# Ten of layer 2's 22 filtered adjacency tiles made during layer 1, two multiplied in the flow ahead of it; a ring of four; roots on GpSimd

## What is computed

```python
# layer 1: three rounds, A = adj scaled by the square roots of the row sums
h1 = x @ W1 + b1
n1 = _layernorm(jax.nn.relu(A @ h1) + h1, g1, be1)
...                                    # two more rounds of the same
# layer 2: only the 700 largest values of a row are kept; seldom more than 700 are there
sim = jnp.tanh(adj * simlar)           # simlar is adj itself
filt = sim * (adj > 0).astype(sim.dtype)
...
h2 = jnp.tanh(h @ W_proj + b_proj)
feat = jax.nn.relu(new_adj @ (h2 @ W_gcn) + b_gcn)
```

## Time and profile before

| | |
|---|---|
| time, median of 3 runs | 2290.98 us (2286.65 to 2292.18) |
| the profiled execution | 2291.57 us, of it the span 2289.7 us |
| PE busy | 1947.9 us, 85% of the span |
| DVE busy | 1574.2 us, 69% |
| ACT busy | 1111.3 us, 49% |
| POOL busy | 443.3 us, 19% |
| DMA | 389.10 MB, mean 170 GB/s |
| granted clock of TensorE | 0.934 mean |

### The profile page before, as it was taken

One profiled execution on the slowest core, in us unless ns is written; L12 is line 12 of the kernel. 1 busy time (PEld: TensorE's weight loads), 2 busy tenths in 40 slices (PEclk: granted clock), 3 DMA queues, 4 the chain that ended last, 5 costly groups with the idle time before them and its releaser, 6 DMA issues.

```text
span 2289.7 us, 42272 instructions
## 1 busy us (share of the span) xinstructions
PE 1947.9 (85%) x15872; PEld 1314.7 (57%) x15872; DVE 1574.2 (69%) x3183; ACT 1111.3 (49%) x2198; POOL 443.3 (19%) x455
## 2 busy tenths in 40 slices
PE   6999296899999999749966698669967999999788
PEld 3877263688888887637744577557754222222343
DVE  6866665655555577746667888645567999999555
ACT  7555275523223244427745677346545223232654
POOL 0000474100000022137741000057620000000000
PEclk9999697999999999969987899879988999999899
DMA  6999367556566589556754567433332343232000
GB/s 197 315 343 328 122 151 163 210 199 246 219 230 243 220 324 404 191 191 218 231 165 133 148 168 179 164 98 93 85 110 73 115 122 90 82 90 85 0 21 29
DMA packets 236971, 389.10 MB, mean 170 GB/s; under 512 B 20640, under 2 KB 189216, under 8 KB 221025
## 3 DMA queue, kind: packets, MB, share of 16 engines
q1 hardware_dynamic: 211972, 333.86, 44.4%
q0 software_dynamic: 15296, 43.88, 7.3%
q10 hardware_dynamic: 9504, 8.65, 1.2%
HBM read 304.55 MB, written 81.78 MB: 169 GB/s over the span
## 4 chain that ended last, share of the span: by engine, by line
PE 51%; DVE 27%; ACT 8%; DMA 8%; issue 4%; POOL 2%; SPq 1%; ACTq 0%; DVEq 0%; POOLq 0%
DVE BIG L2819 7%; PE ps L1078 6%; PE ps L1080 6%; PE ps L1079 6%; PE ps L283 5%; PE ps L284 4%; PE ps L285 4%; PE ps L2320 4%; PE ps L2641 4%; DMA BIG<-in_adjT 3%; PE ps L2647 2%; PE ps L2322 2%; DMA X<-rows_split,idxg 2%; DVE BIG L1735 2%; DVE BIG L1743 2%
## 5 line engine op out<-in xcount | busy, mean ns | idle before, releaser
L1078 PE MATMUL ps<-R,BIG 128*128 128x256 f16 (+1 forms) x1764 | 486.1, 276 | 13.4 <-DVE BIG L1110 8.6
L1080 PE MATMUL ps<-R,BIG 128*128 128x256 f16 (+1 forms) x1764 | 483.5, 274 | 0.0
L1079 PE MATMUL ps<-R,BIG 128*128 128x256 f16 x1764 | 483.4, 274 | 0.0
L2641 PE MATMUL ps<-BIG 128*64 128x452 f32 x1056 | 230.9, 558 | 23.9 <-DVE BIG L2819 20.1
L1078 PEld LDWEIGHTS ps<-R,BIG 128*128 128x128 f16 x1764 | 171.9, 97 | 41.3 <-DVE BIG L1110 9.1
L2819 DVE SCALAR_TENSOR_TENSOR BIG<-BIG 128x904 f32<-128x904 f32 x176 | 192.4, 1155 | 1.6
L1079 PEld LDWEIGHTS ps<-R,BIG 128*128 128x128 f16 x1764 | 173.8, 98 | 21.5
L1080 PEld LDWEIGHTS ps<-R,BIG 128*128 128x128 f16 x1764 | 172.0, 98 | 24.5
L2703 ACT ACTIVATE BIG<-X,BIG 128x64 f32<-128x64 f32 x264 | 70.2, 337 | 232.8 <-PE ps L2647 232.7
L2641 PEld LDWEIGHTS ps<-BIG 128*64 128x64 f32 x1056 | 64.4, 136 | 186.4 <-issue 131.1
L2320 PE MATMUL ps<-BIG,X 128*128 x464 | 155.6, 382 | 9.6 <-DVE X L2379 9.6
(11 more groups left out here) (419 smaller groups left out, 4489.8 us busy)
## 6 DMA issues: line engine op xcount, KB each, us to landing
BIG<-adj_split SPq DMA_DIRECT2D x63, 1376.0 KB, 6.5
BIG<-in_adjT SPq DMA_DIRECT2D x42, 1408.0 KB, 10.8
BIG<-in_adj SPq DMA_DIRECT2D x22, 1408.0 KB, 9.2
BIG<-in_adjT SPq DMA_DIRECT2D x66, 452.0 KB, 3.3
adj_split<-BIG SPq DMA_DIRECT2D x21, 1376.0 KB, 10.9
XX<-in_f SPq DMA_DIRECT2D x70, 256.0 KB, 7.9
experts_split<-XX SPq DMA_DIRECT2D x64, 256.0 KB, 4.4
BIG<-experts_split SPq DMA_DIRECT2D x16, 1024.0 KB, 13.0
```

The costliest lines, as they stand in the source:

```text
L1078: pe.matmul(out[:, 0:n], pr[:, 0, k, :], h[:, k, 0:n], start=start, stop=False)
L1079: pe.matmul(out[:, 0:D], pr[:, 0, k, :], l[:, k, 0:D], start=False, stop=False)
L1080: return pe.matmul(out[:, 0:n], pr[:, 1, k, :], h[:, k, 0:n], start=False, stop=stop)
L2641: pe.matmul(ps[rs, 2 * (h // 2) + c, 0:CW], self.G[:, u, h * HF:(h + 1) * HF], self.PT[:, u, h, cs], start=start, stop=stop)
```

## The change

The tiles of layer 2 are cut in two kinds, `AHEAD` (ten) and `LATE` (twelve). The filter of the AHEAD tiles, which needs only `adjT`, is done in runs 1 and 2 of P1: raw load to slot 5, square on DVE at tile m, tanh on ACT at m+1, high part on ACT and low part on DVE at m+2 into slot 4, and a store to the new DRAM tensor `filter_split`. For that the ring of P1 shrinks from six slots to four, loads waiting for three tiles' lead, and the counting passes move to other places (15 still in runs 1 and 2). P1's roots in runs 1 and 2 go from ACT to POOL, and ACT loads the table with tanh before run 1 and the one with Ln and Exp at the end of run 2. In C1, SP loads tiles 0 to 3 ready-made behind the transfers of rows 6, 9, 12 and 15, and PE multiplies tiles 0 and 1 in its steps from 10 on, block pair by block pair as the features come (`early`). P2 loads the other AHEAD tiles and filters only the twelve LATE ones. The unused branch gets the same ten tiles.

```diff
+RING = 4
+AHEAD = (0, 1, 2, 3, 5, 7, 9, 13, 15, 18)
+LATE = tuple(t for t in range(KT) if t not in AHEAD)
+SQUARES = tuple(4 * i + 2 for i in range(len(AHEAD)))
+COUNTS = tuple(m for m in range(2 * KT) if m % 6 in (1, 3)) + tuple(range(2 * KT + 2, 3 * KT, 3))
...
         class C1:
             def sp(self, sp, filter):
                 after(sp, self.experts, W[2], *self.before)
-                expert_rows(sp, self.st)
+                expert_rows(sp, self.st, {6: lambda: filter.part_load(sp, 0), 9: lambda: filter.part_load(sp, 1),
+                                          12: lambda: filter.part_load(sp, 2), 15: lambda: filter.part_load(sp, 3)})
...                                                            # C1.pe
+                    if i >= 10:
+                        beside.early(pe, i - 10)
...                                                            # C1.act
-                    if i == PR + 5:
-                        filter.first_part(act, 0)
...
         class P1:
             def sp(self, sp):
                 for n in range(3 * KT + 3):
-                    if n < 6:
-                        self.flow.st.wait(sp, "ta", (2, 4, 6, 8, 9, 10)[n])
-                    s.wait(sp, "used", n - 5)
-                    g = n - 2 * KT - 5
+                    if n < RING:
+                        self.flow.st.wait(sp, "ta", (2, 4, 6, 8)[n])
+                    s.wait(sp, "used", n - RING + 1)
+                    g = n - 2 * KT - RING + 1
...
+                    for i in range(len(AHEAD) + 1):
+                        if n == (SQUARES[i - 1] + 7 if i else 3):
+                            s.wait(sp, "lo", i)
+                            if i < len(AHEAD):
+                                self.raw_load(sp, i)
+                            if i:
+                                sp.dma_start(filtered[i - 1], pflat(4, 0, BLOCKS)).then_inc(s["d4"], 16)
...
+            def filter_square(self, v, i):
+                self.st.wait(v, "d5", 16 * i + 16)
+                v.scalar_tensor_tensor(aslot(5), aslot(5), 0.0, aslot(5), ALU.max, ALU.mult).then_inc(self.st["r"], 1)
+
+            def filter_tanh(self, act, i):
+                self.st.wait(act, "r", i + 1)
+                act.activation(aslot(5), aslot(5), ACT.Tanh).then_inc(self.st["h2h"], 1)
+
+            def filter_high(self, act, i):
+                s.wait(act, "h2h", i + 1)
+                s.wait(act, "d4", 16 * i)
+                ac.inc(act.activation(pslot(4)[:, 0], aslot(5), ACT.Copy))
+                stack_high(act, s, pslot(4), aslot(5))
+
+            def filter_low(self, v, i):
+                self.st.wait(v, "hi", i + 1)
+                v.tensor_tensor(pslot(4)[:, 1, 0:KT - 1], aslot(5)[:, 0:KT - 1], pslot(4)[:, 0, 0:KT - 1], ALU.subtract)
+                stack_low(v, pslot(4), aslot(5)).then_inc(self.st["lo"], 1)
...                                                            # P1.act
+                act.preload_act_table_set("exp_and_others")
                 for m in range(2 * KT):
                     raw(m)
                     if self.right_first(m):
                         right(m - 1)
-                    s.wait(act, "ag", m + 1)
-                    root_act(act, m % 4, 1, s)
                     if m % KT == AT - 1:
                         parts_out(act, s, (m + 1) % 2, D, m // KT + 1)
+                    if m - 1 in SQUARES:
+                        self.filter_tanh(act, SQUARES.index(m - 1))
+                    if m - 2 in SQUARES:
+                        self.filter_high(act, SQUARES.index(m - 2))
+                    if m == 2 * KT - 1:
+                        act.preload_act_table_set("natural_log_exp_and_others")
                     high(m)
...
             def pool(self, pool):
+                for m in range(2 * KT):
+                    self.st.wait(pool, "ag", m + 1)
+                    root_pool(pool, m % 4, 1, self.st)
                 LATER.low(pool)
...                                                            # P1.dve
-                    if m % 3 == 1:
-                        count(m // 3)
+                    if m in COUNTS:
+                        count(COUNTS.index(m))
+                    if m in SQUARES:
+                        self.filter_square(v, SQUARES.index(m))
+                    if m - 2 in SQUARES:
+                        self.filter_low(v, SQUARES.index(m - 2))
...
         class P2:
                 def loads(src):
+                    free = [(t - 3, 0, t) for t in AHEAD if t >= 4]
+                    free += [(LATE[j - 3] - 1 if j >= 3 else -3, 1, j) for j in range(len(LATE))]
+                    for _, late, i in sorted(free):
+                        if late:
+                            raw(src, i)
+                        else:
+                            self.part_load(sp, i)
...
+            def early(self, pe, j):
+                self.flow.st.wait(pe, "hl", j + 1)
+                for t in range(2):
+                    for k in (2 * j, 2 * j + 1):
+                        three(pe, ps[:, t, :], pslot(t), k, HAh, HAl, D, k == 0, False)
+                    if j == PR - 1:
+                        pe.matmul(ps[:, t, 0:D], ones16[:, 0:P], bghl[:, :], start=False, stop=True).then_inc(s["used"], 1)
...
             def pe(self, pe):
-                for t in range(KT):
-                    s.wait(pe, "lo", t + 1)
+                for j in range(self.flow.BESIDE, PR):
+                    self.early(pe, j)
+                for t in range(2, KT):
+                    self.split_ready(pe, t)
                     s.wait(pe, "ev", t - 1)
```

More of the change, by code:

```diff
@@ L786, in expert_rows @@
                 sp.dma_start(yg2[:, t % 4, :, :], src[:, :, t, :]).then_inc(s[f"d{t % 4}"], 16)
+                if t in beside:
+                    beside[t]()
         def take_two(v, s, i):
@@ L802, in build @@
         class C1:
+            BESIDE = PR - 2
             GR = -(-PR // 2)
@@ L829, in pool, with pe @@
                     root_pool(pool, 2 * (i % 3), 2, s)
-            def pe(self, pe):
+            def pe(self, pe, beside):
                 s = self.st
@@ L1325, in dve, with __init__ @@
                         rows.bias_out(v, s)
+        class Kept:
+            def __init__(self, *done):
+                self.done = list(done)
         class P1:
@@ L1633, in __init__ @@
                 self.rows = Rows(E1, 4 * D, ["bg", "bias"])
-                self.st = Stage("seq", **{f"d{4 + u}": 16 * len(range(u, KT, 3)) for u in range(3)}, r=KT, nn=KT, zp=1,
-                                hi=KT, lo=KT, used=KT, ev=KT, ag=KT, le=KT, t=KT, qp=1, qs=1, **Rows.totals())
+                L = len(LATE)
+                self.st = Stage("seq", **{f"d{4 + u}": 16 * len(range(u, L, 3)) for u in range(3)},
+                                **{f"w{u}": 16 * len([t for t in AHEAD if t % 4 == u]) for u in range(4)},
+                                r=L, nn=L, zp=1, hi=L, lo=L, used=KT, ev=KT, ag=KT, le=KT, t=KT, qp=1, qs=1, **Rows.totals())
                 self.flow, self.free, self.top = flow, free, top
@@ L1670, in pe @@
                     for k in range(KT):
-                        if t == 0 and k % 2 == 0:
-                            self.flow.st.wait(pe, "hl", k // 2 + 1)
                         if t == AT + 1 and k == 10:
@@ L1713, in act @@
                 s, rows = self.st, self.rows
-                for t in (1, 2):
-                    self.tanh(act, t)
-                    self.first_part(act, t)
                 for t in range(KT + 3):
@@ L1728, in act, with square @@
                 act.preload_act_table_set("natural_log_exp_and_others")
-            def square(self, v, t):
-                s, a = self.st, aslot(4 + t % 3, ORDER[t])
-                s.wait(v, f"d{4 + t % 3}", 16 * (t // 3) + 16)
-                if t == AT:
+            def square(self, v, j):
+                s, a = self.st, aslot(4 + j % 3, ORDER[LATE[j]])
+                s.wait(v, f"d{4 + j % 3}", 16 * (j // 3) + 16)
+                if LATE[j] == AT:
                     s.wait(v, "zp", 1)
@@ L1738, in dve, with split @@
                 s, rows = self.st, self.rows
-                def split(t):
-                    s.wait(v, "hi", t + 1)
-                    pr, a = pslot(t % 4, ORDER[t]), aslot(4 + t % 3, ORDER[t])
+                def split(j):
+                    t = LATE[j]
+                    s.wait(v, "hi", j + 1)
+                    pr, a = pslot(t % 4, ORDER[t]), aslot(4 + j % 3, ORDER[t])
                     v.tensor_tensor(pr[:, 1, 0:KT - 1], a[:, 0:KT - 1], pr[:, 0, 0:KT - 1], ALU.subtract)
                     stack_low(v, pr, a).then_inc(s["lo"], 1)
-                split(0)
-                self.square(v, 1)
-                self.square(v, 2)
-                split(1)
-                self.square(v, 3)
                 for t in range(KT + 2):
@@ L1761, in dve @@
                         newton(v, (t - 2) % 4, 1).then_inc(s["rs"], 1)
-                    if t + 2 < KT:
-                        split(t + 2)
```

(14 more changed lines are left out.)

200 lines of the change are left out of this document (119 added, 81 removed).

## The result

The changed kernel takes **2277.6 us** (median of 5 runs, 2271.24 to 2279.14) against 2291.0 for the kernel before (5 runs on the same chip, 2286.65 to 2292.18): ratio 0.9939, 95% interval 0.9921 to 0.9956. It is faster, by 13.4 us where 30 were forecast. The profiled execution took 2279.14 us, its span is 2277.3, the mean granted clock 0.937. Every ratio is to that kernel; between kernels of different groups it is the fairer measure, as a difference of their medians can be off by a microsecond or more.

A forecast was written before the change was run, and what follows sets the result against it. P2 was taken as bound by DVE in its filter, P1 by PE with DVE and ACT half idle. Terms -47 + 5 + 4 + 4 + 2 + 2 = -30 on 2291.57 gave 2261 us, range 2243 to 2283.

The forecast's parts named there:

- third rival: C1: `early` costs 11.8 us and the transfers 12, in place of 9 together; total 2276 us, chance 10%.
- P2, -47 forecast: P2 falls from 199.9 to 152.8 us: start 2.5, 19 tiles at 7.70 each, short tile 4.
- Does PE set it?: P2: PE sets the pace at 7.70 us per tile; DVE has 115 us in 153, working two tiles ahead.
- The short tile was put at 4: P2's short tile takes 4 us, between 3 and 6 beside a full one, taken from run 3.
- The start was put at 2.5: P2's start: the last block pairs, two steps of 12 matmuls, with bias and the taking, 2.5 us.
- C1, +9 forecast: C1 grows by 5 us for `early` in PE's order and 4 for split-tile loads among the expert rows.
- `early` at +5: C1: 9 of 11 steps, 11.8 us, enter PE's order; what its waits don't hold costs 5, between 0 and 11.8.
- The loads' +4: C1: big transfers make rows 7 and 13 each 2 or 3 us late; 4 us, between 0 and 18.
- The first part of tile 0: C1: ACT no longer makes this part, 2.5 us; costed at nothing, as the last matmul isn't done before.
- P1, runs 1 and 2, +4 forecast: P1: added filter work and POOL's roots cost 4 us, between -1 and +10; DVE needs 29.2 of 32.8 us per four tiles.
- second rival: P1: the raw load lands late, its square begins 3 us late in nine periods; 21 us, total 2282, chance 13%.
- Run 3 and the tables: P1: run 3's ring load 56 or 57 is close, +2 us, between 0 and +10; ACT's two table loads together +2.

The follow-up runs named there:

- experiment 8: Changed kernel with the first load of ACT's table moved from ahead of P1's first product into C0: 2273.1 us, ratio 0.9929 to the kernel before.

## Why the prediction was right or wrong

The gain came, but less than half of the forecast. By the spans: P2 gave 16 us less than forecast and runs 1 and 2 of P1 lost 5 more, while C1 lost 4 less and run 3 one less. The time lies within 2243 to 2283, and beside the 2276 of the third rival, "C1 pays in full"; that is luck, as C1 paid less than the forecast and P2 made the difference.

**P2, -47 forecast, -31.0 measured: the step that failed.** It was "Does PE set it?", ending in "I find no second limit". It added up each engine's work over P2 (DVE 115 of 153 us, ACT 12 x 5.2) and let DVE's two tiles of lead cover the peaks. The loads were right: DVE's 31.72 of 50 us is 63%, ACT's 28.38 57%. But the rows, unlike the filter, have no lead of two tiles; each passes PE, ACT, DVE and PE within its tile, in the engines' written order, behind 5.4 us of tanh and high part. By terms: 19 full tiles were put at 7.70 and took 8.02 on the mean, 152.4 in place of 146.3, +6.1. The short tile was put at 4 and took 12.5 (12.31 + 8.27 + 8.06 over three takings, less two tiles of 8.06), as it waits for a round of the ring like a full one, +8.5. PE waits 2.67 us for the row ahead of it (1360.84) and 3.70 for the one in the tile behind (1369.01); then its granted clock is low for a while, its matmuls 0.21 us apart in place of 0.11:

```profile
1369.00:1373.00 4.00, 3.99 (x21) 2.54 (x22) 0.19 (x1) 0.60 (x1) 0.00 (x0) 0.59 0.12 37
```

That is an estimated 1.6 us of the 8.5 (0.41 of 4 us). The 4 us had been taken from run 3, while the kernel before has a step of 12.58 us at this very tile in P2, with waits of 2.67 and 3.71 beside it.

The start was put at 2.5 and took 3.9, +1.4. With ScalarE's order changed, the 19 tiles are at 7.70 on the mean, which leaves 6.0 for the short one, and P2 is within 3.4 us of the 152.8 forecast: the step's arithmetic stands, its "if" did not. It could have been read from the code of the kernel before, in the order of ACT's steps in P2 (away, tanh, first part, row), and from its trace, where PE waits for that row 14 times; I had looked at DVE alone there, since it had no waits.

**C1, +9 forecast, +5.4 measured.** `early` at +5 was right (5.3). The loads' +4 was drawn from the right mechanism, two waits at the rows 7 and 13 of 1.9 us (2 or 3 said), but these reach C1's end by half, some 2. The first part of tile 0 that leaves ACT in C1 (2.5 us, 2.9 with its last block) was costed at nothing, with the last matmul as the reason; the last features did wait for it, and 0.7 us are shown to come back. The other 1.3 by which the kernel without either addition is shorter stay open. On the transfers queued in one ring, the Trainium skill ("DMA: Bandwidth & Descriptors", section Queues, rings and completion order) says that an engine takes one ring's descriptors in order; the two waits agree, as both stand at the row issued right behind a big load.

**P1, runs 1 and 2, +4 forecast, +9.3 measured**, within its -1 to +10. The root on POOL took 0.4 us more and not 0.2, worth 2.9 us in all, 1.8 of them around the short tiles. The balance per four tiles was right in the steady part, which lost nothing. The text named the spot, "behind the short tile, where two products come 4 us apart", but its sum let the next free tile give the time back; it does not, for PE has by then waited. The steps there are 7.2 us longer, the 1.8 of the roots included, and moving the work off these tiles gave 6.1 of them back. In the second rival the text's own terms give 12.1 + 4.5 - 12.5 = 4.1 us late, not 3; it didn't come about.

**Run 3 and the tables.** +2 forecast, +0.7 measured for run 3, within what it varies by. For the tables +2 forecast, and no more than a microsecond shown (experiment 8): a load is 1.28 us in the row, the one at the end of run 2 stands in a gap. The Trainium skill ("ScalarE: Activation LUTs", section What ACT_TABLE_LOAD costs) gives 1283 ns for the load and 1380 ns for a drain; the row agrees with the first, while nothing is seen of the second, as ACT's next instruction begins 1.30 us after the load began. The second rival of the text, a late raw load, did not come: DVE never waits for `in_adjT` in P1. Transfers of runs 1 and 2, after:

```profile
BIG<-adj_split SPq DMA_DIRECT2D x41, 1376.0 KB, 6.9
BIG<-in_adj SPq DMA_DIRECT2D x14, 1408.0 KB, 9.6
filter_split<-BIG SPq DMA_DIRECT2D x10, 1376.0 KB, 12.8
BIG<-in_adjT SPq DMA_DIRECT2D x9, 1408.0 KB, 10.2
```

The raw load lands in 10.2 us where 11 to 12 were expected and 12.5 allowed.

**Left open.** The +2.2 us in the rest and -1.5 in the experts, which the change doesn't touch, have no cause that a run shows; other kernels of the changed form had 823.1 to 826.2 in the rest, those of the form before 823.9 to 824.9. Whether `early` pays more once P2 runs at PE's pace was not tried.

## What to carry to other kernels

Before costing work taken off the busiest engine at the next engine's pace, follow one unit of work round all engines in their written order and add up what stands in that ring: here the limit behind the first one was a ring in which no engine is full, and its work was moved out of it by order alone. A short wait that the second engine already repeats, tile by tile, was its sign. Put work with slack behind work that someone waits for, but not behind a wait that it doesn't need itself. Where tiles are of unequal length, spread added work by the time that passes there and keep it off the short one; an average over tiles hides that.

## What the runs showed of the hardware

A root handed from DVE to POOL and back took 0.99 to 1.06 us of waiting, through ACT 0.60. A table load took 1.28 us, and ACT's next instruction began 0.02 us behind it. TensorE's granted clock was 1.00 while it was busy all of 1300 to 1350 us; in the changed kernel, once it had waited 2.67 and 3.70 us within 9 us, the clock was 0.59 over the next 4 us, the lower level of 0.50 for most of them. In P1's first run the DMA engines moved 286 GB/s at a share of 0.79 where they had 223 at 0.60, and loads of 1376 KB landed in 6.9 us where they had 6.1.
